# The last cycles of a six-layer attention stack in an order of their own, with the output's normalisation inside them

## The chip, the core and the metric

One core of one Trainium2 chip runs the whole kernel. The core has five engines with a queue of instructions each: PE (matrix multiplication and transposes; its weight loads run beside it), ACT (functions and copies), DVE (vector arithmetic and reductions), POOL (vector arithmetic, slower) and SP, which here only issues DMAs. They meet through semaphores. The metric is the device time of one execution in microseconds; lower is better. A measurement of this kernel is uncertain by about 0.2%.

## What is computed

The input x is 8 sequences of 512 tokens of 128 numbers. The reference, cut to what matters:

```
x = x + layernorm(L0_attn_ref(layernorm(x), Wq, ..., bo))
x = x + layernorm(L0_ffn_ref(layernorm(x), Wqkv, ..., b2))

# L0_ffn_ref
for i in range(6):
    x = attn_layer(shift_tokens(x), Wqkv[i], q_scale[i], k_scale[i], Wo[i]) + x
    x = ffn_layer(shift_tokens(x), ln_g[i], ln_b[i], W1[i], b1[i], W2[i], b2[i]) + x
```

`attn_layer` has 16 heads of 64: q and k are normalised, turned by rotary tables, and each window of 32 tokens looks at itself and the window before. `ffn_layer` is a layer normalisation, a gated product with an exact gelu and a second product. What the change touches is the end: the last cycles of layer 6, and the last line, the normalisation of the stack's result and the addition of the residual.

## The kernel before

The kernel has three stages: `mqa_stage` (the first attention; it also writes its result, the residual, to DRAM), `layers_stage` (the six layers) and `output_stage`. Inside the layers, x stays in SBUF, transposed, as `xT`.

**Cycles.** A tile is 128 tokens; a sequence has 4 tiles, a half has 2 (`PER`). A cycle works on one half at each of many steps, so a layer has 16 cycles (`STEPS`) and a sequence two. The table `CYCLE` writes down, engine by engine, in what order the steps of a cycle stand, each with the tile that it is for, counted from the cycle's first:

```
CYCLE = {
    "PE": "Tq:0 aPq:2 mean bPq:2 Tk:0 V:-2 aPk:2 var bPk:2 S:0 spread X:-1 aPv:2 O:-2 bPv:2 Tq:1 V:-1 Tk:1 "
    "aPq:3 O:-1 bPq:3 GG S:1 AA aPk:3 bPk:3 W:-1 aPv:3 X:0 bPv:3 F4",
...
    "DVE": "XC aCq:2 bCq:2 Rq:2 FV R:-2 aCk:2 XM bCk:2 MX:0 RS:-1 SB:0 R:-1 Rk:2 aCq:3 bCq:3 MX:1 Rq:3 AM "
    "aCk:3 bCk:3 WX:-1 RS:0 SB:1 XN Rk:3",
```

In the text, a step's number is its tile or half in the last layer: S:30 is S for tile 30 of 0 to 31 (cycle 15 is the one that begins with Tq:30), XN:14 is the FFN's last step for half 14. The steps on PE: P projects to q, k, v (three matmuls each, into `proj`); Tq and Tk transpose q and k; S makes the scores (128 pairs of weight load and matmul of 64x64); X transposes the probabilities; V weights the values (128 such pairs); O transposes the attention's result; W is the output projection. The FFN follows two cycles behind (`LAG`): mean, var and spread for its normalisation, GG and AA the two halves of the first product, F4 the second. On the others: DVE has C and R of the rotation and l2 norm, MX and SB before the exponential, RS the denominators, R the weighting, WX and XN the two additions to `xT`, XC, FV, XM, AM in the FFN; ACT copies out of PSUM (EQ, EK, EX, EO, EV, XF, XH) and computes EXP and GEL; POOL has A, M, N of the rotation and norms, FP (a power of -1/2), XL and Xl; SP has VM, which moves a tile's values to `v_win` by ten DMAs.

**What sets the order.** Each engine runs its row of the table in order, and a step first waits for its inputs' semaphores. The outputs of most steps of PE go to a ring of two PSUM tensors (`ring`, `take`), so a step also waits until the reader of the last user of its slot is done (`RELEASE`). `steps_of` leaves out, at both ends, the steps whose tile does not exist: so the last cycles are the same row with gaps. PE runs its cycles in a loop (`Fori`) up to cycle 13 of the last layer; cycles 14 to 17 stand behind it as straight code. The other engines have loops of their own (`run`, `middle`), which end there too. At the end of each layer's turn of its loop SP loads the next layer's weights (`new_layer`), which in the sixth layer there is nothing of.

**The output stage** starts behind a barrier of all engines. SP loads the whole residual (2 MB) in one DMA. PE transposes all 8 sequences into 8 PSUM banks. Then, per sequence, DVE computes statistics and variance, POOL the power -1/2, DVE the normalised tiles, POOL adds them to the residual, and SP sends it out. The steps of one sequence stand beside those of the next.

## Time and profile before

| | us |
|---|---|
| median of three runs | 3441.85 (3436.19 to 3443.91) |
| the profiled execution | 3438.51 |
| its span, first to last instruction | 3436.8 |
| PE busy | 3273.3 (95%) |
| DVE busy | 2964.5 (86%) |
| ACT busy | 2734.5 (80%) |
| POOL busy | 2616.0 (76%) |
| mean granted TensorE clock | 0.984 of full speed |

A profile is one execution: each instruction has a start and a duration, from the span's start. "Busy" is the time in which an engine had an instruction under way. The idle time ahead of an instruction stands in brackets with what ended it; "issue" means that the profile shows nothing that the engine waited for. PEld is PE's weight load. The granted clock is 1.00 at full speed and 0.50 when PE runs at half of it.

### The profile page before, as it was taken

To read this page: it belongs to the slowest core of one execution; us is meant where nothing else is said; L and a number is where in the kernel's file an instruction comes from. 1 tells how busy PE (TensorE), PEld (TensorE's weight loads), DVE (VectorE), ACT (ScalarE), POOL (GpSimd) and SP (SyncE) were. 2 spreads that over 40 slices of the span, in tenths; PEclk is the share of its full clock that TensorE was granted. 3 is DMA by queue.
4 is the path that set the end of the run, shared out by engine and by line. 5 is a ranking of instruction groups with operands and counts; after the bars stand their busy time and mean duration, and the time that the engine had idled before them with its cause. 6 is when DMAs were issued, how large, how long until landed. Compare 5 with 4: busy or idle time off the path is not lost. (4 is left out here: it accounts for less than half of the span.)

```text
span 3436.8 us, 161363 instructions
## 1 busy us (share of the span) xinstructions
PE 3273.3 (95%) x66105; PEld 2798.2 (81%) x66106; DVE 2964.5 (86%) x5351; ACT 2734.5 (80%) x4522; POOL 2616.0 (76%) x3358
## 2 busy tenths in 40 slices
PE   7999679999999999999999999999999999999994
PEld 5767458888888888888888888888888888888883
DVE  7777578999999999989999999999999999999974
ACT  4777458888888888888888888888888888888872
POOL 5677577777887777887778787778778778778762
PEclk9999889999999999999999999999999999999997
DMA  2000013222223222232222232222232222222221
GB/s 61 4 8 8 16 51 99 74 69 66 64 77 99 73 70 65 71 94 74 73 73 62 74 92 73 73 73 61 75 92 73 73 73 68 69 66 73 73 67 59
DMA packets 161797, 228.61 MB, mean 67 GB/s; under 512 B 42264, under 2 KB 60640, under 8 KB 161504
## 3 DMA queue, kind: packets, MB, share of 16 engines
q1 hardware_dynamic: 161632, 226.85, 24.6%
q8 instruction: 49, 0.80, 0.1%
q14 instruction: 116, 0.95, 0.1%
HBM read 21.00 MB, written 4.19 MB: 7 GB/s over the span
## 5 line engine op out<-in xcount | busy, mean ns | idle before, releaser
L1184 POOL TENSOR_TENSOR by_cos<-by_cos,by_sin 128x1024 f32<-128x1024 f32 x384 | 913.9, 2390 | 0.0
L1190 POOL TENSOR_TENSOR by_cos<-by_cos,norms 128x1024 f32<-128x1024 f32 x384 | 729.6, 1911 | 0.0
L1560 DVE TENSOR_TENSOR by_cos<-proj,turns 128x512 f32<-128x512 f32 x768 | 523.9, 682 | 72.3 <-ACT squares L1446 67.9
L1289 PE MATMUL proj<-qkv_hi,xs_hib 128*128 128x512 f32 x1152 | 559.7, 486 | 25.7 <-DVE by_sin L1562 12.9
L1562 DVE TENSOR_TENSOR by_sin<-proj,turns 128x512 f32<-128x512 f32 x768 | 521.5, 679 | 0.0
L1446 ACT ACTIVATE squares<-proj 128x512 f32<-128x512 f32 x768 | 443.1, 592 | 42.7 <-DVE sumsb L1566 16.1
L1566 DVE TENSOR_REDUCE sumsb<-squares 128x16 f32<-128x1024 f32 x384 | 464.1, 1209 | 0.0
L1291 PE MATMUL proj<-qkv_hi,xs_lob 128*128 128x512 f32 x1152 | 458.9, 398 | 0.7 <-issue 0.7
L1290 PE MATMUL proj<-qkv_lo,xs_hib 128*128 128x512 f32 x1152 | 456.2, 396 | 0.0
L1298 PE MATMUL ring<-ident,by_cos 128*128 128x128 f32 x3072 | 405.9, 275 | 8.8 <-ACT pTb L1425 4.5
L1298 PEld LDWEIGHTS ring<-ident,by_cos 128*128 128x128 f32 x3072 | 351.5, 141 | 57.7 <-issue 9.6
L1352 PE MATMUL ring<-attnT,wo 128*128 128x256 f32 x1536 | 347.2, 379 | 0.6 <-ACT hidden L1529 0.6
L1317 PEld LDWEIGHTS score<-kTb,qTb 64*32 64x32 f32 x24576 | 278.9, 105 | 62.8 <-issue 40.3
L1352 PEld LDWEIGHTS ring<-attnT,wo 128*128 128x128 f32 x1536 | 291.7, 190 | 43.7 <-ACT hidden L1529 0.8
L1317 PE MATMUL score<-kTb,qTb 64*32 64x64 f32 x24576 | 320.8, 226 | 4.2 <-issue 3.9
L1425 ACT ACTIVATE pTb<-ring 128x1024 f32<-128x1024 f32 x192 | 196.9, 1026 | 160.3 <-PE ring L1324 157.3
L1168 POOL TENSOR_TENSOR newton_b<-norms 128x32 f32<-128x32 f32 x384 | 91.8, 239 | 294.4 <-ACT norms L1457 279.4
L1425 ACT ACTIVATE qTb<-ring 128x1024 f32<-128x1024 f32 x192 | 197.0, 1026 | 139.4 <-PE ring L1298 139.3
L1338 PE MATMUL ring<-v_win,pTb 64*32 64x64 f32 x24576 | 286.6, 226 | 9.3 <-issue 9.3
L742 DVE CUSTOM_DVE_ANT_0 a_masked<-a_score,a_mask_qk 128x512 f32<-128x512 f32 (+3 forms) x512 | 229.5, 487 | 72.3 <-PE a_score L390 65.0
L1338 PEld LDWEIGHTS ring<-v_win,pTb 64*32 64x32 f32 x24576 | 254.8, 105 | 42.7 <-issue 42.7
L1575 DVE TENSOR_REDUCE row_maxb<-score 128x16 f32<-128x1024 f32 x192 | 234.0, 1219 | 52.6 <-PE score L1317 52.5
(190 smaller groups left out, 7850.3 us busy)
## 6 DMA issues: line engine op xcount, KB each, us to landing
v_win<-vb SPq DMA_DIRECT2D x1152, 128.0 KB
v_win<-vb SPq DMA_DIRECT2D x768, 64.0 KB
in_qkv<-L_ffn_Wqkv SPq DMA_DIRECT2D x12, 768.0 KB
wo<-L_ffn_Wo SPq DMA_DIRECT2D x6, 512.0 KB, 4.1
x_tok<-L_attn_x SPq DMA_DIRECT2D x8, 256.0 KB, 4.4
residual<-x_tok SPq DMA_DIRECT2D x8, 256.0 KB, 2.0
o_x<-residual SPq DMA_DIRECT2D x1, 2048.0 KB, 8.5
out<-o_x SPq DMA_DIRECT2D x8, 256.0 KB, 2.2
```

The source lines that it names most:

```text
L1184: nc.gpsimd.tensor_tensor(both, both, by_sin[:, j, :], ALU.add).then_inc(e[f"{w_}_added"].sem, 1)
L1190: nc.gpsimd.tensor_tensor(heads, heads, inverse, ALU.mult).then_inc(e[f"{w_}_ready"].sem, 1)
L1289: nc.tensor.matmul(out, xs_hi[:, tile], qkv_hi[:, cols], start=True, stop=False)
L1290: nc.tensor.matmul(out, xs_hi[:, tile], qkv_lo[:, cols], start=False, stop=False)
L1291: nc.tensor.matmul(out, xs_lo[:, tile], qkv_hi[:, cols], start=False, stop=True)\
L1298: last = nc.tensor.transpose(out[:, i * P:(i + 1) * P], by_cos[:, t % 2, j, i * P:(i + 1) * P], ident[:, :])
L1317: last = nc.tensor.matmul(score[queries, at:at + KEYS], qT[rows, t % 2, i, queries], keys, start=False, stop=True, skip_group_check=True)
L1338: last = nc.tensor.matmul(out[queries, at:at + DH], pT[rows, i, queries], v_win[rows, t % 2, n, i, :], start=True, stop=True)
L1352: last = nc.tensor.matmul(out[:, 0:HS], wo[:, i, :], attnT[:, i, :], start=(i == 0), stop=(i == PAIRS - 1))
L1560: nc.vector.tensor_tensor(of_heads(by_cos[:, t % 2, j, cols]), heads, table(0), ALU.mult)
L1562: nc.vector.tensor_tensor(swapped, heads, table(1), ALU.mult).then_inc(e[f"{w_}_rotated"].sem, 1)
L1566: nc.vector.tensor_reduce(sums[:, t % 2, j, :, 0], squares[:, :].rearrange("p (h d) -> p h d", d=DH), AX.X, ALU.add).then_inc(e[f"{w_}_sum ...
```

## The change

Two things are put together. First, the last layer's last cycles no longer come from `CYCLE` with gaps: a new table, `LAST`, has a row of its own for each engine for all that is left from cycle 15 on, with the same steps in nearly the same order. `last_steps` reads it. Cycle 14 now is the last one of `CYCLE`, and on PE it runs in the loop, which goes one cycle further. Second, `output_stage` is gone. Its work is cut in nine units (`UNITS`): sequences 0 to 6, and the two halves of sequence 7. Five kinds of step of each stand inside the rows of `LAST`: Y (PE transposes the unit's tiles into one half of `proj`, by turns), YS (DVE: statistics and variance), YR (POOL: power), YN (DVE: normalised into a half of `squares`), YA (POOL: addition). Y:u waits, from u = 2 on, until YN:(u-2) is done. The residual is loaded by SP once the last layer's weights have been converted, into the space of the loaded weights and of the rotary tables (`in_qkv`, `tables`): two DMAs, 2 MB together, at the place where other layers load weights. The additions are made there, and the outputs sent from there as units become ready, behind all of SP's VM steps. There is no barrier between the layers and the output.

The core of the diff:

```diff
+UNITS = [(b, 0, TILES) for b in range(B - 1)] + [(B - 1, h * PER, PER) for h in range(HALVES)]
+LAST = {
+    "PE": "Tq:30 mean:13 Y:0 Y:1 Tk:30 V:28 var:13 S:30 spread:13 X:29 O:28 Tq:31 V:29 Tk:31 Y:2 O:29 GG:13 "
+    "S:31 AA:13 W:29 X:30 F4:13 mean:14 Y:3 V:30 var:14 spread:14 X:31 O:30 GG:14 V:31 O:31 Y:4 AA:14 W:31 Y:5 "
+    "F4:14 mean:15 Y:6 var:15 spread:15 GG:15 Y:7 AA:15 F4:15 Y:8",
...
+}
...
-def layers_stage(nc, c, e, w, arrived):
+def layers_stage(nc, c, e, w, arrived, residual, out_dram):
...
+            last_layer()
             middle(DEPTH - 1)
-            for at in range(STEPS - HALVES, STEPS + HALVES * LAG):
-                cycle(((DEPTH - 1) * STEPS, at), None, DEPTH - 1, at, 0, PER * STEPS)
+            base = (DEPTH - 1) * STEPS
+            for at in range(STEPS - HALVES, STEPS - 1):
+                cycle((base, at), None, DEPTH - 1, at, 0, PER * STEPS)
+            for at, s_, t, token in last_steps(name):
+                step(s_, t, token, (base, at), None, DEPTH - 1)
...
+            def last_layer():
+                for x in p_lo:
+                    sp.wait_ge(p_lo[x], DEPTH)
+                sp.wait_ge(p_turns, DEPTH * 4)
+                sp.sem_inc(sp_ready, 1)
+                sp.dma_start(in_qkv[:, :].rearrange("p (n d) -> p n d", d=D), residual[:, 0:AT_ONCE * TILES, :])\
+                    .then_inc(x_loaded, 16)
...
+            run(sp, "SP", step, new_layer, last_layer)
+            for u, (b, first, n) in enumerate(UNITS):
+                sp.wait_ge(summed, u + 1)
+                sp.dma_start(out_dram[b].rearrange("(t p) d -> p t d", p=P)[:, first:first + n, :],
+                             residual_of(u).rearrange("p (t d) -> p t d", d=D)).then_inc(stored, 16)
...
+                elif kind == "YR":
+                    n = UNITS[t][2]
+                    pool.wait_ge(var_done, t + 1)
+                    nc.gpsimd.tensor_tensor(o_rstd[:, t % 2, 0:n], o_var[:, t % 2, 0:n], c["minus_half"][:, 0:n],
+                                            ALU.pow).then_inc(rstd_done, 1)
+                elif kind == "YA":
+                    pool.wait_ge(x_loaded, 32)
+                    pool.wait_ge(normalised, t + 1)
+                    nc.gpsimd.tensor_tensor(residual_of(t), residual_of(t), normal_of(t), ALU.add).then_inc(summed, 1)
...
+                elif kind == "Y":
+                    b, first, n = UNITS[t]
+                    half = HALVES * b + (first + n) // PER - 1
+                    pe.wait_ge(e["x_new"].sem, e["x_new"].at(half + 1, (DEPTH - 1) * STEPS))
+                    if t < 2:
+                        pe.wait_ge(e["v"].sem, e["v"].at(PER * STEPS, (DEPTH - 1) * STEPS))
+                    else:
+                        pe.wait_ge(normalised, t - 1)
+                    for i in range(n):
+                        at = 1 + (first + i) * P
+                        last = nc.tensor.transpose(turned_of(t)[:, i * P:(i + 1) * P], c["xT"][:, b, at:at + P], ident[:, :])
+                    last.then_inc(turned, 1)
...
-            with nc.Fori(LAG, DEPTH * STEPS - HALVES, engines=one, hint_back_edge=True) as n:
+            with nc.Fori(LAG, DEPTH * STEPS - 1, engines=one, hint_back_edge=True) as n:
                 cycle(n)
...
+                elif kind == "YN":
+                    dve.wait_ge(rstd_done, t + 1)
+                    if t >= 2:
+                        dve.wait_ge(summed, t - 1)
+                    for i in range(UNITS[t][2]):
+                        tile = slice(i * P, (i + 1) * P)
+                        last = nc.vector.tensor_scalar(normal_of(t)[:, tile], turned_of(t)[:, tile], stat[:, t % 2, i, 0:1],
+                                                       o_rstd[:, t % 2, i:i + 1], ALU.subtract, ALU.mult)
...
-def output_stage(nc, c, residual, out_dram):
...
-        layers_stage(nc, c, layers, ffn_inputs, arrived)
-        output_stage(nc, c, residual, out_dram)
+        layers_stage(nc, c, layers, ffn_inputs, arrived, residual, out_dram)
```

The rows of `LAST` of the other engines, for cycle 16 and 17 (from XN:13 on DVE): "XN:13 XC:14 SB:31 FV:14 R:30 XM:14 RS:31 YN:2 R:31 YS:3 YS:4 YN:3 AM:14 YN:4 WX:31 YS:5 XN:14 XC:15 FV:15 XM:15 YN:5 YS:6 YS:7 AM:15 YN:6 XN:15 YS:8 YN:7 YN:8"; ACT: "XF:14 EX:30 FSQ:14 EXP:31 XH:14 EX:31 EO:30 GEL:14 EO:31 XF:15 FSQ:15 XH:15 GEL:15".

Three places of the order that results. PE where its loop ends, before (`COMPARE_AND_BRANCH` is the loop's end; L1289 to L1291 with `proj` are the projections, L1298 is Tq or Tk, L1338 V, L1362 mean, L1393 F4):

```order
L1393 MATMUL ring<-hidden,w 128x256 x3
L1415 REGISTER_ALU
L1415 COMPARE_AND_BRANCH
L1298 MATMUL ring<-ident,by_cos 128x128 x8
L1289 MATMUL proj<-qkv_hi,xs_hib 128x512
L1290 MATMUL proj<-qkv_lo,xs_hib 128x512
L1291 MATMUL proj<-qkv_hi,xs_lob 128x512
L1362 MATMUL ring<-xfb,mean_of 128x256
```

and PE where its loop ends, after the change (L1376 is Tq or Tk, L1443 is Y, L1416 V, L1458 var, L1395 S, L1465 spread):

```order
L1505 COMPARE_AND_BRANCH
L1376 MATMUL ring<-ident,by_cos 128x128 x8
L1452 MATMUL ring<-xfb,mean_of 128x256
L1443 MATMUL proj<-ident,xT 128x128 x8
L1376 MATMUL ring<-ident,by_cos 128x128 x8
L1416 MATMUL ring<-v_win,pTb 32x64 x64
L1458 MATMUL ring<-mean_of,fsqb 128x1 x2
L1395 MATMUL score<-kTb,qTb 32x64 x64
L1465 MATMUL ring<-ident,f_rstdb 128x128 x2
```

Cycle 14, with its projections, is no longer behind the loop; what follows it is cycle 15, with the transposes of Y:0 and Y:1 ahead of Tk:30.

PE in cycle 16, before: from spread:14 over X:31, O:30, V:31, O:31 to the first rows of GG:14.

```order
L1375 MATMUL ring<-ident,f_rstdb 128x128 x2
L1324 MATMUL ring<-ident,probs 128x128 x8
L1345 MATMUL ring<-ident,attnb 128x128 x8
L1338 MATMUL ring<-v_win,pTb 32x64 x64
L1345 MATMUL ring<-ident,attnb 128x128 x8
L1384 MATMUL ring<-xn_hib,w_hi 128x256
```

and after the change, from O:30 over GG:14 (the rows L1474 to L1476, of which there are nine), V:31, O:31 and Y:4 to the first row of AA:14:

```order
L1423 MATMUL ring<-ident,attnb 128x128 x8
L1474 MATMUL ring<-xn_hib,w_hi 128x256
...
L1416 MATMUL ring<-v_win,pTb 32x64 x64
L1423 MATMUL ring<-ident,attnb 128x128 x8
L1443 MATMUL proj<-ident,xT 128x128 x4
L1474 MATMUL ring<-xn_hib,w_hi 128x256
```

GG:14 has moved ahead of V:31, and Y:4 stands behind O:31.

DVE at the program's end, after the change: from XM:15 (L1741) over YN:5 (L1723), YS:6 and YS:7 to AM:15 (L1749), YN:6, XN:15 (L1755) and the last unit.

```order
L1741 TENSOR_TENSOR xcb<-xcb,ring 128x256
L1723 TENSOR_SCALAR squares<-proj,o_stat,o_rstd 128x128 x4
L1708 BN_STATS o_stat<-proj 128x6 x4
L1712 BN_AGGR o_stat<-o_stat 128x2 x4
L1715 TENSOR_SCALAR o_var<-o_stat 128x4
...
L1749 SCALAR_TENSOR_TENSOR hidden<-ring,ffn_col,hidden 85x256
L1723 TENSOR_SCALAR squares<-proj,o_stat,o_rstd 128x128 x4
L1755 TENSOR_TENSOR xT<-ring,xT 128x256
L1708 BN_STATS o_stat<-proj 128x6 x2
L1712 BN_AGGR o_stat<-o_stat 128x2 x2
L1715 TENSOR_SCALAR o_var<-o_stat 128x2
L1723 TENSOR_SCALAR squares<-proj,o_stat,o_rstd 128x128 x4
```

Before, XM:15, AM:15 and XN:15 followed each other directly, and all eight sequences' statistics stood behind XN:15; now only the last unit's do, and the normalisation of the last two.

## Rows read from the trace of the kernel before

**Rows 1.** Chain that ended last, in order of time: start us, us, what.

```profile
3404.31 8.49 DMA o_x<-residual
...
3432.87 1.27 POOLq L1647
```

**Rows 2.** Timeline of the output stage: start us, us, engine, line, operation, out<-in, count [idle].

```profile
3404.82 3.22 PE L1666 MATMUL o_turn<-ident,xT 128*128 128x128 f32 x28
...
3417.89 0.88 DVE L1690 BATCH_NORM_STATS2 o_stat<-o_turn 128x6 f32<-128x128 f32 x4
...
3418.80 0.38 DVE L1694 BATCH_NORM_AGGREGATE o_stat<-o_stat 128x2 f32<-128x6 f32 x4
3419.22 0.17 DVE L1697 TENSOR_SCALAR o_var<-o_stat 128x4 f32<-128x4 f32 x1
3419.31 1.37 DVE L1703 TENSOR_SCALAR o_o<-o_turn,o_stat,o_rstd 128x128 f32<-128x128 f32 x4
3419.47 1.02 POOL L1676 TENSOR_TENSOR o_rstd<-o_var,minus_half 128x4 f32<-128x4 f32 x1 [0.16 <-DVE o_var L1697]
```

**Rows 3.** Busy us by stretch, XN to XN: cycles 15, 13, 14, 16, 17.

```profile
3329.90:3359.80 29.90, 24.70 (x624) 21.90 (x621) 13.81 (x20) 17.89 (x23) 8.63 (x14) 0.89 0.28 73
3267.40:3297.30 29.90, 29.90 (x661) 26.21 (x660) 27.36 (x41) 25.47 (x40) 23.52 (x30) 1.00 0.27 71
3297.30:3329.90 32.60, 30.62 (x663) 26.34 (x662) 27.41 (x41) 24.84 (x38) 23.70 (x29) 1.00 0.26 68
3359.80:3390.20 30.40, 20.04 (x328) 16.85 (x328) 6.93 (x14) 9.80 (x15) 1.97 (x3) 0.72 0.01 2
3390.20:3403.60 13.40, 7.13 (x32) 5.62 (x32) 2.66 (x8) 4.98 (x8) 1.98 (x3) 0.75 0.00 0
```

(The columns: stretch, its us, then PE, PEld, DVE, ACT, POOL with their instructions, granted clock, DMA share, GB/s.)

**Rows 4.** The page's groups: S (L1317) and V (L1338), busy, mean ns | idle.

```profile
L1317 PE MATMUL score<-kTb,qTb 64*32 64x64 f32 x24576 | 320.8, 226 | 4.2 <-issue 3.9
...
L1338 PE MATMUL ring<-v_win,pTb 64*32 64x64 f32 x24576 | 286.6, 226 | 9.3 <-issue 9.3
```

**Rows 5.** Timeline of PE: the waits for "issue" inside S and V.

```profile
3307.88 0.32 PE L1317 MATMUL score<-kTb,qTb 64*32 64x64 f32 x10 [1.27 <-issue]
...
3335.49 0.43 PE L1338 MATMUL ring<-v_win,pTb 64*32 64x64 f32 x24 [1.34 <-issue]
...
3339.56 0.67 PE L1317 MATMUL score<-kTb,qTb 64*32 64x64 f32 x29 [1.94 <-issue]
...
3365.26 0.37 PE L1338 MATMUL ring<-v_win,pTb 64*32 64x64 f32 x2 [1.96 <-issue]
...
3376.55 0.66 PE L1338 MATMUL ring<-v_win,pTb 64*32 64x64 f32 x26 [2.42 <-issue]
```

**Rows 6.** Timelines of PE, POOL and DVE in cycles 15 to 17.

```profile
3331.84 1.09 PE L1298 MATMUL ring<-ident,by_cos 128*128 128x128 f32 x8 [0.74 <-ACT qTb L1425]
...
3384.32 3.72 PE L1352 MATMUL ring<-attnT,wo 128*128 128x256 f32 x16 [0.57 <-ACT hidden L1529]
3388.55 1.56 PE L1393 MATMUL ring<-hidden,w 128*128 128x256 f32 x6 [0.52 <-DVE xT L1603]
...
3393.24 0.71 POOL L1213 TENSOR_TENSOR f_rstdb<-f_varb,minus_half 128x2 f32<-128x2 f32 x1 [20.77 <-DVE f_varb L1622]
...
3396.87 0.55 PE L1384 MATMUL ring<-xn_hib,w_hi 128*128 128x256 f32 x1 [2.17 <-POOL xn_lob L1209]
...
3400.61 1.26 DVE L1634 SCALAR_TENSOR_TENSOR hidden<-ring,ffn_col,hidden 128x256 f32<-128x256 f32 x3 [5.46 <-PE ring L1386]
3403.59 0.42 DVE L1640 TENSOR_TENSOR xT<-ring,xT 128x256 f32<-128x256 f32 x1 [1.72 <-PE ring L1393]
```

**Rows 7.** Timeline of SP in a layer before: the weights' load, and the next VM.

```profile
2503.02 0.87 SPq L936 DMA_DIRECT2D in_qkv<-L_ffn_Wqkv  x2
...
2516.74 0.55 SPq L1128 DMA_DIRECT2D v_win<-vb  x1
```

**Rows 8.** POOL's additions in the output stage: ns min/median/max, first and last start.

```profile
L1682 POOL TENSOR_TENSOR o_x<-o_x,o_o x8: 1259/1260/1262, 3415.4 to 3432.9; 128x512 f32<-128x512 f32 x8
```

**Rows 9.** The page's DMA issues: the outputs, KB each, median us to landing.

```profile
out<-o_x SPq DMA_DIRECT2D x8, 256.0 KB, 2.2
```

More of the change, by code:

```diff
@@ L906, in steps_of, with last_steps @@
     return steps
+def last_steps(engine):
+    at = STEPS - 1
+    for token in LAST[engine].split():
+        name, _, n = token.partition(":")
+        if name in OUTPUT:
+            yield at, (name,), int(n), ""
+            continue
+        same = [(t, x) for x, kind, t in tokens(engine) if kind == name and (name in FFN or (int(n) - t) % PER == 0)]
+        t, steady = same[0]
+        at = int(n) + LAG if name in FFN else (int(n) - t) // PER
+        yield at, (name,), t, steady
 def layer_events(sem):
```

109 lines of the change are left out of this document (41 added, 68 removed), and 8 rows, old and new, of the table LAST.

## The prediction

> **What bounds the kernel now.** Three views, in this order. First the chain that ended last: it shows that behind the last cycle stands a stage of its own, from 3404.01 us (end of the last XN [rows 6]) to the span's end at 3436.8, so 32.8 us. It begins with a wait of 8.49 us for the DMA that fetches the residual [rows 1], and then goes round eight times: statistics, variance, power, normalisation, addition, on DVE and POOL by turns, while PE and ACT do nothing. The eight additions begin between 3415.4 and 3432.9, so a round is 2.5 us (its parts are in [rows 2, 8]). Second the busy time by stretch, cut at the XN of each cycle [rows 3]: cycle 13, the last that PE takes from its loop, has 29.90 us with PE busy all through. Cycle 14 has the same number of matmuls, but 32.60. From cycle 15 on PE is no longer full (24.70 of 29.90, then 20.04 of 30.40, then 7.13 of 13.40), because the pipeline runs empty: each step waits for the one before it. There is free time on every engine, DVE above all (13.81 of 29.90, 6.93 of 30.40). Third the idle time put down to "issue" on PE [rows 4, 5], below.
>
> **The wait for instructions.** Over the whole run S waited 3.9 us for "issue" in 24576 matmuls and V 9.3 us [rows 4], and most of that lies behind PE's loop: 1.27 and 1.94 in S, 1.34, 1.96 and 2.42 in V [rows 5]. Between the stall at the pair 105 of V:28 and the one at pair 100 of S:30 stand 24 + 4 + 99 pairs and two waits: 256 instructions (a pair is a weight load and a matmul). All five stalls fit a mark every 256 instructions, of which one is 570 behind the loop's exit, at pair 119 of S:28. The closest two stalls end 4.1 us apart (3335.49 to 3339.56), and a tile of V or S, 256 instructions, takes only some 1.5 to 1.8 us without one. So a mark costs 1.3 to 2.4 us where V or S lies between it and the last one, and nothing elsewhere. In the loop there is no such wait.
>
> The Trainium skill, "Runtime: NRT & Kernel Launch", section "Instruction fetch mechanics", has the same 256 instructions (16 KiB blocks, the next fetched while one is executed), and says that passing a block costs little, "mostly hidden". The rows disagree on the cost: 1.3 to 2.4 us each. By the page the term for cycle 14 below would be nought and the marks without a price (rival E).
>
> **The change, part by part.** All against the profiled execution (span 3436.8).
> 1. The output stage goes: -32.8.
> 2. What comes behind XN:15 instead is the half-sequence unit 8. Two transposes and their delay 0.4; two statistics (4 take 0.88), two aggregates (4 take 0.38) and the variance 0.17, with gaps 1.0 (half of a round's, the variance whole); power of 128x2, 0.71 as the FFN's [rows 6]; normalisation of two tiles, half of 1.37, 0.7; addition of 128x256, between half of 1.26 and that, taken 0.7; output DMA and end, as now from 3434.14 (end of the last addition) to 3436.8, 2.7 [rows 1, 2, 8]. With five hand-overs of 0.07 us: +6.6. YN:7 (0.7) lies beside the power, YA:7 beside YN:8. Bounds: 6 to 8.5, if they do not.
> 3. Cycle 14 of PE now runs in the loop (the loop ends one cycle later). The twin of it is cycle 13: 32.60 - 29.90 = -2.7; I take -2.5, since some of the first stalls stay behind the exit. Bounds -2.7 and 0, the latter if the stalls hit cycle 15 instead and nothing covers them.
> 4. Cycle 15. Y:0 and Y:1 (28 transposes took 3.22 us, so 0.5 us for four, 0.6 with their delay) come ahead of Tk:30, which waited 0.74 us for ACT's copy [rows 2, 6]: +0.4. Y:2 stands ahead of O:29, which waits for DVE's R:29: nothing. With the Y's the marks of 256 fall elsewhere. Counted on the rows of the order: at the last pair of V:28, pair 122 of S:30, pair 94 of V:29, pair 62 of S:31 (long after the last one: free). Three stalls, of 1.9, 1.9 and about 1, instead of 1.34 and 1.94: +1.5, of which the waits for ACT and DVE in Tq:31 and O:29 take some: +0.6. Together +1.0, between 0 and +3.
> 5. Cycle 16. The mark moves to pair 13 of V:30 with nothing dense before it, so V:30's 1.96 goes, less Y:3's 0.5 ahead of it: -1.4. V:31 keeps a stall of about 1.9 (pair 107). GG:14 goes from behind O:31 to ahead of V:31, and XH:14 ahead of EX:31 on ACT: GG and AA together lie between 3396.87 and AM's 3400.61 in the last cycle [rows 6], so GG alone costs up to 1.9 us; I take it that V:31 starts 1.5 us later, but behind O:31 stand only Y:4 and AA:14 instead of GG and AA, and W:31 no longer waits for the gelu (0.57 [rows 6]). Net of that move -0.6. Sum -2.0, but a V:31 that is late by more takes it back: between -4.5 and +1.
> 6. The end of cycle 16: Y:5 (0.6 us) comes between W:31 and F4:14, YS:5 (1.4) on DVE between WX:31 and XN:14. F4 started 0.5 us behind W's end (3388.04 to 3388.55) and takes 1.6 [rows 6], which covers both but for a little: +0.2. SB:31 behind XC:14, YN:3 and YN:4 lie in idle time of DVE.
> 7. Cycle 17: YN:5, YS:6 and YS:7 (1.4 + 1.5 + 0.8 = 3.7) must fit in the 5.46 us that DVE is idle before AM:15, YN:6 (1.4) in the 1.72 before XN:15 [rows 6]; both fit. Y:7 between GG and AA: +0.3. If that cover fails, each us is a us.
> 8. The residual's load, 2 MB in 8.49 us, moves to cycle 4 of the last layer, on SP's queue ahead of VM. It waits for events that are past by then. At that place the other layers load Wqkv and the FFN's weights: issued from 2503.02, next VM at 2516.74 [rows 7]. The 13.7 us cover the 8.5. Cost 0; if they did not, VM and V behind it would be late once, by 1 or 2 us. The outputs 0 to 6 leave SP beside PE's work, at 2.2 us each [rows 9]: 0.
>
> On POOL the additions (1.26) and powers (1.02) go into idle time: POOL is busy 8.63 of 29.90 and 1.97 of 30.40 us there [rows 3]. POOL's additions last 1259 to 1262 ns in all eight rounds [rows 8], the last one with DVE idle, the others beside its statistics, so I add nothing. If they were slowed beside DVE's additions in the cycles, only the last two have a waiting reader.
>
> The clock: the granted share is 0.89, 0.72 and 0.75 in the last three stretches [rows 3], that is PE falls to the lower of its levels (1.2 instead of 2.4 GHz) after its idle stretches. I take it that it does so as often. If the Y's keep PE busier at the right moments, or the stalls lie worse, transposes, W, GG and AA of cycle 16 and 17 (some 20 us of PE) take up to 3 us less or 5 more.
>
> Sum: -32.8 + 6.6 - 2.5 + 1.0 - 2.0 + 0.2 + 0.3 = -29.2. Span 3407.6. The profiled execution took 3438.5, 1.7 over its span and 3.3 under the median of the three runs (3441.85); the four times shown (3436.2 to 3443.9) have a mean of 3440.1. I set the change against that mean: 3410.9, and 0.6 for the register and wait instructions of the new steps: 3411.5.
>
> **Rivals.**
> A. *The tail becomes denser.* V:30 and V:31 both escape their marks and the clock stays up: XN:15 comes 4 to 8 us earlier. For it: cycle 16 has 10 us of idle PE, and V:31, R:31 and O:31, one behind the other, set its end. Against: the count above puts a mark in V:31. 3403 to 3407.
> B. *The stalls and the clock eat it.* Five marks in dense places instead of four, the Y's in front of V, and the slow clock over W:31 and GG:15 (W 3.7 us now, twice that at 1.2 GHz): 5 to 10 us later. 3416 to 3422.
> C. *Slower than before.* The Y's have two halves of proj, and Y:u waits on PE, in order, for the normalisation of u-2. If that wait ran the full chain each time (transposes 0.6, statistics 1.5, power 1.02, normalisation 1.37 = 4.5 us, a little more at the lower clock, and all of PE's work behind it), the seven units that wait would cost 32 to 36 us, against 29.2 saved: 3443 to 3447. It decides with the seventh unit. Against: each Y stands several us of other work behind the YN that it waits for; DVE and POOL have the time.
> D. *It does not do what it says*: the gain of the stage given back by item 2 being as long as now, since the addition or output queues behind the earlier ones on SP. At 2.2 us per DMA and one issue each 0.4 us I see only 1 or 2 us: inside the range.
>
> E. *The marks have no price.* If the waits for "issue" were chance and not code that has to come, cycle 14 would keep its 32.6 us in the loop too, and items 3 to 5 would come to nought but for the Y's: -32.8 + 6.6 + 0.8 (item 4 and 5's Y's) + 0.5 = -24.9, 3415 to 3416. Against: 256 between them, five times.
>
> **How the numbers follow.** Forecast (3407 to 3415) 0.62, A 0.14, B 0.15, C 0.01, E 0.05, something that leaves it within 7 us of before (D among it) 0.03. The range, A's and B's middle included and the 4 us between executions of one kernel: 3403 to 3420. A measurement tells about 0.2% (7 us) from no change: faster 0.96, same 0.03, slower 0.01.
>
> **What would show it.** Cycle 14 in 30 us instead of 32.6 (item 3). "Issue" before S and V only behind that, at the pairs named. No wait of DVE for a power ahead of MX:31, AM or XN. From XN:15's end to the span's end 6.6 us. The out DMAs of units 0 to 5 before cycle 17. PE waiting in Y for normalised would make it wrong, and so would XN:14 more than 2 us later than now, set against XN:12.

## Result, and the profile after

The changed kernel took 3408.79 us (median of four executions, 3406.70 to 3409.57), the kernel before beside it 3442.88 us (3436.19 to 3447.51): ratio 0.9897, 95% interval 0.9885 to 0.991. The profiled execution took 3406.7 us, its span is 3405.0 (before: 3438.5 and 3436.8). The prediction was 3411.5, between 3403 and 3420. The stretches did not come out as it said, though: its terms for cycles 15 and 16 were wrong in size, in opposite directions, and that they nearly cancel in the sum is luck.

Busy time by stretch in the changed kernel, from XN to XN: cycles 13 to 17, then all that stands behind the start of XN:15. The columns are those of [rows 3].

```profile
3264.30:3294.20 29.90, 29.90 (x662) 26.10 (x661) 27.37 (x41) 25.50 (x40) 23.53 (x30) 1.00 0.27 71
3294.20:3324.50 30.30, 30.30 (x663) 26.42 (x662) 27.39 (x41) 24.88 (x39) 23.71 (x29) 1.00 0.26 70
3324.50:3360.30 35.80, 27.75 (x636) 24.60 (x633) 19.55 (x55) 17.26 (x23) 14.11 (x19) 0.81 0.28 76
3360.30:3384.30 24.00, 18.32 (x340) 15.30 (x340) 15.99 (x53) 10.15 (x16) 5.41 (x7) 0.93 0.04 13
3384.30:3398.40 14.10, 8.27 (x38) 6.82 (x38) 7.61 (x30) 4.98 (x8) 8.59 (x10) 0.76 0.18 56
3398.40:3405.00 6.60, 0.44 (x2) 0.21 (x2) 2.63 (x10) 0.00 (x0) 3.04 (x4) 0.74 0.25 79
```

Against [rows 3]: cycle 14 has 30.3 instead of 32.6, cycle 15 35.8 instead of 29.9 (1.0 more was forecast), cycle 16 24.0 instead of 30.4 (2.0 less was forecast), with a granted clock of 0.93 where it was 0.72. POOL and DVE now do the output's work in cycles 15 to 17 (DVE 19.55 and 15.99 instead of 13.81 and 6.93). Behind the start of XN:15 stand 6.6 us instead of 33.2. The last 3.1 us of the 31.8 by which the spans differ lie ahead of cycle 14, where PE's order was not edited: the first addition to `xT` (the first WX; the expectations below call it the first XN) stands 1.4 us sooner, the layers from there up to cycle 13 take 1.7 less.

The page's groups of S and V in the changed kernel (busy, mean ns | idle before), for [rows 4]; S waits less for "issue", V more:

```profile
L1395 PE MATMUL score<-kTb,qTb 64*32 64x64 f32 x24576 | 320.9, 226 | 1.9 <-issue 1.5
...
L1416 PE MATMUL ring<-v_win,pTb 64*32 64x64 f32 x24576 | 286.3, 226 | 10.4 <-issue 10.3
```

The waits themselves, from PE's timeline, for [rows 5] (start, us, [idle ahead of it]):

```profile
3330.33 2.02 PE L1416 MATMUL ring<-v_win,pTb 64*32 64x64 f32 x127 [2.75 <-issue]
3334.09 0.26 PE L1416 MATMUL ring<-v_win,pTb 64*32 64x64 f32 x1 [1.74 <-issue]
3338.46 0.43 PE L1395 MATMUL score<-kTb,qTb 64*32 64x64 f32 x6 [1.23 <-issue]
3347.47 0.54 PE L1416 MATMUL ring<-v_win,pTb 64*32 64x64 f32 x35 [2.21 <-issue]
3372.15 0.42 PE L1416 MATMUL ring<-v_win,pTb 64*32 64x64 f32 x22 [1.75 <-issue]
```

A group "x35" is the last 35 pairs of a tile of 128, so it begins at pair 94. The last four stand where the prediction put them, to within one pair (last pair of V:28, pair 123 of S:30 for 122, pair 94 of V:29, pair 107 of V:31), and V:30 and S:31 have none. The first, 2.75 us ahead of V:28, was not forecast. It is the mark at 58 instructions behind the loop's exit, which had cost nothing in the trace of before.

The end of the program, from the timeline of all engines:

```profile
3398.33 0.42 DVE L1755 TENSOR_TENSOR xT<-ring,xT 128x256 f32<-128x256 f32 x1 [0.45 <-PE ring L1483]
3398.81 0.21 PEld L1443 LDWEIGHTS proj<-ident,xT 128*128 128x128 f32 x2 [0.92 <-DVE xT L1755]
...
3399.29 0.49 DVE L1708 BATCH_NORM_STATS2 o_stat<-proj 128x6 f32<-128x128 f32 x2 [0.54 <-PE proj L1443]
...
3400.35 0.71 POOL L1283 TENSOR_TENSOR o_rstd<-o_var,minus_half 128x2 f32<-128x2 f32 x1 [1.06 <-DVE o_var L1715]
...
3401.97 0.72 POOL L1288 TENSOR_TENSOR tables_sb<-tables_sb,squares 128x256 f32<-128x256 f32 x1 [0.19 <-DVE squares L1723]
```

One unit goes through the chain that eight sequences went through before [rows 2]: transposes 3398.81, addition at 3401.97, span's end 3405.0.

One sign that the prediction named did not come: of the output DMAs of units 0 to 5 only three were issued before cycle 17 (3355.57, 3357.35 and 3377.73 us), the next three in it (3386.42 to 3393.25). Nothing waits for them but the end of the program, which the last unit's sets.

### The profile page after: what moved, and what is told of

It is laid out like the page before. It is cut to its first block, busy times and chain, and to the rows that moved or that the text cites. A ratio compares the mean times of both kernels' runs of the same rounds, so it can differ in the third digit from the quotient of the medians.

```text
span 3405.0 us, 161393 instructions
## 1 busy us (share of the span) xinstructions
PE 3269.8 (96%) x66106; PEld 2794.3 (82%) x66106; DVE 2966.7 (87%) x5352; ACT 2734.6 (80%) x4522; POOL 2616.7 (77%) x3360
## 4 chain that ended last, share of the span: by engine, by line
POOL 38%; issue 32%; PE 15%; POOLq 2%; DVE 1%; ACT 1%; SPq 0%; DVEq 0%; ACTq 0%; DMA 0%
POOL by_cos L1253 12%; POOL by_cos L1259 9%; POOL newton_b L1239 2%; POOL newton_b L1241 2%; POOL norms L1243 2%; POOL newton_b L1237 2%; POOL xs_lob L1267 2%; POOL xn_lob L1278 2%; PE ring L1376 2%; POOL f_rstdb L1291 2%; PE ring L1430 2%; PE score L1395 1%; PE ring L1416 1%; PE proj L1367 1%; POOLq L1059 1%
## 5 line engine op out<-in xcount | busy, mean ns | idle before, releaser
L1376 PE MATMUL ring<-ident,by_cos 128*128 128x128 f32 x3072 | 405.5, 275 | 7.8 <-ACT pTb L1518 4.5
L1376 PEld LDWEIGHTS ring<-ident,by_cos 128*128 128x128 f32 x3072 | 351.4, 141 | 56.4 <-issue 9.4
L1395 PEld LDWEIGHTS score<-kTb,qTb 64*32 64x32 f32 x24576 | 278.9, 105 | 59.9 <-issue 37.2
L1395 PE MATMUL score<-kTb,qTb 64*32 64x64 f32 x24576 | 320.9, 226 | 1.9 <-issue 1.5
L1416 PE MATMUL ring<-v_win,pTb 64*32 64x64 f32 x24576 | 286.3, 226 | 10.4 <-issue 10.3
L1416 PEld LDWEIGHTS ring<-v_win,pTb 64*32 64x32 f32 x24576 | 254.5, 105 | 41.5 <-issue 41.3
```

What stands on the lines that cost most here:

```text
L1376: last = nc.tensor.transpose(out[:, i * P:(i + 1) * P], by_cos[:, t % 2, j, i * P:(i + 1) * P], ident[:, :])
L1395: last = nc.tensor.matmul(score[queries, at:at + KEYS], qT[rows, t % 2, i, queries], keys, start=False, stop=True, skip_group_check=True)
L1416: last = nc.tensor.matmul(out[queries, at:at + DH], pT[rows, i, queries], v_win[rows, t % 2, n, i, :], start=True, stop=True)
```

## Experiments

All were measured beside runs of the kernel before, in five sessions, not all on one chip; the medians of the kernel before lie between 3442.88 and 3443.80 us in all of them. "Tail" is the time from the start of XN:11 (the end of cycle 13) to the span's end, in one trace; "marks" is the sum of the waits for "issue" at marks in it; the waits of 0.56 and 1.22 ahead of V:30's and V:31's first pairs in cycle 16, there in both traces of before, are not among them, nor are 0.27 and 0.35 ahead of V:29 in e9 and e11 (no code block was under way at any of these: the last packet had left 7.5 to 10.3 us before they ended). "Ahead" says whether the first code block behind PE's loop was fetched before the exit (16 KB packets of PE's instruction queue in the trace). Each tail is that of one traced execution, and it need not be the median one: e1's was the slowest of its nine (3441.89 us) and e5's of its four, the changed kernel's first and e10's were the fastest of their four.

| kernel | median us (n) | tail | cycle 14 | 15 and 16 | 17 | from XN:15 | marks | ahead |
|---|---|---|---|---|---|---|---|---|
| before | 3442.88 (4) | 139.5 | 32.6 | 60.3 | 13.4 | 33.2 | 9.6 | yes |
| before again, e8 | 3443.07 (1) | 143.5 | 36.2 | 60.5 | 13.5 | 33.2 | 11.0 | no |
| changed | 3408.79 (4) | 110.8 | 30.3 | 59.8 | 14.1 | 6.6 | 9.7 | no |
| changed again, e9 | 3409.56 (4) | 108.5 | 30.3 | 57.4 | 14.2 | 6.6 | 7.8 | yes |
| e1 loop only | 3435.95 (9) | 139.0 | 30.2 | 61.3 | 15.1 | 32.4 | 7.1 | no |
| e2 all behind | 3435.83 (11) | 136.6 | 30.3 | 58.1 | 13.7 | 34.6 | 5.5 | no |
| e6 behind, four | 3429.46 (7) | 129.8 | 30.4 | 58.7 | 13.7 | 27.0 | 6.3 | no |
| e3 GG late | 3412.33 (4) | 113.8 | 30.2 | 62.5 | 14.1 | 6.9 | 9.1 | no |
| e7 short loop | 3412.43 (4) | 111.2 | 35.5 | 54.8 | 14.2 | 6.7 | 9.1 | no |
| e4 shift at start | 3408.45 (4) | 104.9 | 30.3 | 52.2 | 15.5 | 6.9 | 4.3 | no |
| e5 shift spread | 3398.47 (4) | 104.6 | 30.3 | 51.9 | 15.5 | 6.9 | 3.9 | no |
| e10 the same again | 3398.19 (4) | 101.4 | 30.3 | 48.7 | 15.5 | 6.9 | 3.0 | yes |
| e12 shift by 28 | 3405.61 (4) | 104.8 | 30.3 | 53.8 | 14.1 | 6.6 | 7.0 | no |
| e11 no hint | 3405.41 (4) | 106.8 | 30.3 | 56.0 | 13.9 | 6.6 | 8.0 | (kept) |

**The longer loop alone (e1).** Before, with

```
-            with nc.Fori(LAG, DEPTH * STEPS - HALVES, engines=one, hint_back_edge=True) as n:
+            with nc.Fori(LAG, DEPTH * STEPS - 1, engines=one, hint_back_edge=True) as n:
...
-            for at in range(STEPS - HALVES, STEPS + HALVES):
+            for at in range(STEPS - 1, STEPS + HALVES):
```

> The kernel before with one edit: PE's loop ends one cycle later, so that cycle 14 of the last layer runs in it; output stage and order as before. Theory (stalls for code at marks of 256 instructions, the first 58 behind the loop's exit): cycle 14 takes 30.3 us instead of 32.6. The marks behind the exit then fall at pair 9 of V:28, pair 3 of S:30, the start of X:29, pair 103 of V:29 and pair 75 of S:31, and at sparse places from there on: stalls of about 2.7, 1.9, 1.9 and 0.9 us in cycle 15 and none in V:30 and V:31, where before had 1.96 and 2.42. Cycle 15 longer by 4, cycle 16 shorter by 4 us. In all -2.5 us against before. Rival (the first mark is free when no Y stands in front of V:28, as it was in before): no stall at V:28, cycle 15 longer by 1.5 only, in all -5 us. Rival (the wait moves with V's and S's, not with the marks): V:30 and V:31 keep their 1.96 and 2.42.

Measured: 3435.95 us, ratio to before 0.9976 (0.9966 to 0.9986), so 5 to 12 us less by the interval: more than the theory's 2.5, with the rival's 5 at its edge. The marks are where the count put them. PE's timeline of e1:

```profile
3337.26 1.97 PE L1338 MATMUL ring<-v_win,pTb 64*32 64x64 f32 x120 [2.62 <-issue]
3341.13 2.03 PE L1317 MATMUL score<-kTb,qTb 64*32 64x64 f32 x125 [0.61 <-issue]
3345.26 1.87 PE L1324 MATMUL ring<-ident,probs 128*128 128x128 f32 x8 [1.49 <-issue]
3353.99 0.66 PE L1338 MATMUL ring<-v_win,pTb 64*32 64x64 f32 x26 [2.42 <-issue]
```

So V:28 is stalled without any Y in front of it: "the first mark is free" falls, and so does "the wait moves with V and S". The size was explained only by e8: set against its tail of 143.5, e1's 139.0 is 4.5 us less.

**The kernel before once more (e8).**

> The kernel before once more, for a second trace: how much of the difference between two traces lies in stretches that no edit touches. From the span's start to the first XN and from there to the last layer's cycle 13 the traces so far (without the one with 104 increments at the start) differ by 4 and by 3 us. Expected: the stalls for issue at the same pairs as in the first trace of this kernel (pair 118 of S:28, 105 of V:28, 100 of S:30, V:30 and V:31), their lengths within 0.7 us, and the stretch from XN:12 to the end 105 to 109 us, moved by the granted clock. The other reading (stalls for issue are chance) would put them elsewhere.

Measured: 3443.07 us. PE's timeline of this second trace:

```profile
3304.00 1.47 PE L1338 MATMUL ring<-v_win,pTb 64*32 64x64 f32 x126 [2.40 <-issue]
3307.47 0.79 PE L1291 MATMUL proj<-qkv_hi,xs_lob 128*128 128x512 f32 x1 [0.85 <-issue]
...
3340.00 0.43 PE L1338 MATMUL ring<-v_win,pTb 64*32 64x64 f32 x24 [1.61 <-issue]
3343.80 0.67 PE L1317 MATMUL score<-kTb,qTb 64*32 64x64 f32 x29 [1.67 <-issue]
```

Pair 105 of V:28 and pair 100 of S:30 again. But S:28 has none, and at pair 3 of V:26, the mark at 58 behind the exit, stand 2.40 us that the first trace did not have. In the first trace the block behind the exit was fetched at 3295.48, 1.6 us ahead of the exit; in this one at 3301.38, when PE came to the mark. Cycle 14 took 36.2 us here and 32.6 there. The prediction sized its term for cycle 14 on the rarer of two cases: of the 14 traces it is in three, the other one in ten, and in e11 the block needed no fetch.

**Only the order of GG:14 (e3).** PE of the changed kernel, with XH:14 and GEL:14 put back on ACT too:

```
-    "S:31 AA:13 W:29 X:30 F4:13 mean:14 Y:3 V:30 var:14 spread:14 X:31 O:30 GG:14 V:31 O:31 Y:4 AA:14 W:31 Y:5 "
+    "S:31 AA:13 W:29 X:30 F4:13 mean:14 Y:3 V:30 var:14 spread:14 X:31 O:30 V:31 O:31 Y:4 GG:14 AA:14 W:31 Y:5 "
```

> The changed kernel with GG:14 put back behind O:31 and Y:4 on PE, and XH:14 behind EX:31 and GEL:14 behind EO:31 on ACT, as in the kernel before; all else as in the changed one. Theory (the record's -0.6 us for this move): total +0.6 us, V:31 starts about 1.5 us sooner and W:31 waits 0.5 us for the gelu again; XN:13 to XN:14 24.5 us instead of 23.9. Rival (the move is what brought cycle 16 its 6.4 us, by keeping PE busy between V:30 and V:31 and its clock up): XN:13 to XN:14 27 us or more, granted clock well under 0.93 there, total +3 or more. Rival (V:31's start sets the end): total -1 us.

Measured: 3412.33 us (3409.28 to 3414.21, the changed kernel 3406.70 to 3409.57), its tail 3.0 longer, cycle 16 26.1 instead of 23.9; of the rest, 0.6 lies in cycle 15, ahead of the edit's place on PE. PE's timeline, first e3, then the changed kernel, at V:31:

```profile
3371.32 1.04 PE L1417 MATMUL ring<-ident,attnb 128*128 128x128 f32 x8
3374.10 1.38 PE L1410 MATMUL ring<-v_win,pTb 64*32 64x64 f32 x116 [1.75 <-ACT attnT L1512]
...
3382.22 0.41 PE L1469 MATMUL ring<-xn_lob,w_hi 128*128 128x256 f32 x1
```

```profile
3366.51 1.04 PE L1423 MATMUL ring<-ident,attnb 128*128 128x128 f32 x8
3367.85 0.39 PE L1474 MATMUL ring<-xn_hib,w_hi 128*128 128x256 f32 x1 [0.30 <-ACT pTb L1518]
...
3369.10 1.30 PE L1416 MATMUL ring<-v_win,pTb 64*32 64x64 f32 x106
```

V:31 waits 1.75 us for ACT's copy of O:30 when nothing stands in front of it. GG:14 fits into that wait: from O:30's start to V:31's start are 2.78 us without GG and 2.59 with it. The prediction had V:31 come 1.5 us later for it, although the first trace of the kernel before has a wait at the same place, put down to "issue" there:

```profile
3372.92 1.21 PE L1338 MATMUL ring<-v_win,pTb 64*32 64x64 f32 x102 [1.22 <-issue]
```

Behind O:31, GG and AA run 14 of their 18 matmuls at 0.41 us each, at the lower clock, where the changed kernel has mostly 0.28. The stalls' places and sums are nearly the same (9.1 and 9.7), so the 2.2 us of cycle 16 are GG's place with the clock there (0.87 instead of 0.93), by one trace of each.

**All the output behind XN:15 (e2), and with four places (e6).** e2 keeps the early load of the residual, has no stage and no barrier, and puts the 45 output steps last; all other steps stand in the order of the kernel before, GG:14 behind O:31 too (cut):

```
-    "F4:14 mean:15 Y:6 var:15 spread:15 GG:15 Y:7 AA:15 F4:15 Y:8",
+    "F4:14 mean:15 var:15 spread:15 GG:15 AA:15 F4:15 Y:0 Y:1 Y:2 Y:3 Y:4 Y:5 Y:6 Y:7 Y:8",
...
+    "AM:15 XN:15 YS:0 YS:1 YN:0 YS:2 YN:1 YS:3 YN:2 YS:4 YN:3 YS:5 YN:4 YS:6 YN:5 YS:7 YN:6 YS:8 YN:7 YN:8",
```

> The changed kernel with the nine output units Y, YS, YR, YN, YA all behind XN:15, and everything else in the last cycles in the order of the kernel before. The residual is still loaded in cycle 4 of the last layer and there is no stage boundary. Theory: the 8.5 us of waiting for the residual go, the eight rounds stay, so XN:15's end to the span's end is 24 to 25 us instead of 32.8 (before) and 6.3 (after); up to XN:15 as the kernel with the longer loop alone. Total about 11 us under before, near 3430 us, 22 us over after. Rival (the load is not what sets it, since the first statistics run beside it anyway): 29 to 30 us behind XN:15, total near 3435. Rival (Y's two halves of proj cost a full chain of 4.5 us each): 36 us or more behind XN:15, total at or over before's.

Measured: 3435.83 us, the same as e1, and 34.1 us from XN:15's end, so the early load brought nothing here. A round in e2's timeline, the first Y that has to wait and the next:

```profile
3402.91 1.09 PE L1437 MATMUL proj<-ident,xT 128*128 128x128 f32 x4 [3.94 <-DVE squares L1717]
3404.03 0.89 DVE L1702 BATCH_NORM_STATS2 o_stat<-proj 128x6 f32<-128x128 f32 x4 [1.27 <-PE proj L1437]
...
3406.96 1.08 PE L1437 MATMUL proj<-ident,xT 128*128 128x128 f32 x4 [2.96 <-DVE squares L1717]
```

A round is 4.06 us, because Y:u stands behind the normalisation of u-2. This is rival C's chain (4.5 us by its estimate), measured where nothing covers it. e6 uses four places of PSUM, and the first four units also wait until `score` is free (cut):

```
-            return proj[:, u % 2 * 512:u % 2 * 512 + UNITS[u][2] * P]
+            return (proj, score)[u // 2 % 2][:, u % 2 * 512:u % 2 * 512 + UNITS[u][2] * P]
...
-                        pe.wait_ge(normalised, t - 1)
+                        pe.wait_ge(normalised, t - 3)
```

> The kernel with all output units behind XN:15, but with four places in PSUM for the turned tiles (the two halves of proj and the two of score) instead of two, so that Y:u waits for the normalisation of unit u-4. With two places XN:15's end to the span's end took 34.1 us: seven waits on PE of 3 us, a round of 4.06 us. Theory (the two places were what ate the 8.5 us of the early load): rounds at DVE's pace, 2.8 to 2.9 us, 26 to 27.5 us behind XN:15, total 7 us under the kernel with two places. Rival (the addition's or the power's wait on POOL sets the round): unchanged, 34 us. The record's 6.6 us behind XN:15 is not touched by either.

Measured: 3429.46 us, 26.5 us from XN:15's end, rounds of 2.70 us. So the early load and the missing barrier are worth 32.8 - 26.5 = 6.3 us once Y's wait no longer sets the round, two places of PSUM instead of four take 7.6 (34.1 - 26.5), and having all but unit 8 inside the cycles is worth the remaining 20.3 (26.5 to 6.2).

**The short loop (e7).** The changed kernel with cycle 14 as straight code again:

```
-            with nc.Fori(LAG, DEPTH * STEPS - 1, engines=one, hint_back_edge=True) as n:
+            with nc.Fori(LAG, DEPTH * STEPS - HALVES, engines=one, hint_back_edge=True) as n:
...
+            cycle((DEPTH - 1) * STEPS + STEPS - HALVES, STEPS - HALVES, 0, PER * STEPS)
```

> The changed kernel with PE's loop ending one cycle sooner, as in the kernel before: cycle 14 of the last layer is straight code again. By the record (cycle 14 is worth 2.5 us, all else stays): 2.5 us slower than the changed kernel. Theory now (the sum of the stalls counts, and the marks move by 1344 instructions modulo 256): cycle 14 takes 32.6 us again, but the marks fall at pair 95 of V:28, pair 90 of S:30, pair 61 of V:29, pair 29 of S:31, X:30, pair 108 of V:30 and pair 74 of V:31, and the first mark behind the loop's exit was fetched ahead in the kernel before, so V:28 loses its 2.75 and pays 1.2 to 1.3; S:30 1.9, V:29 0 to 1, V:30 and V:31 nearly nothing. Stalls 6 to 7 us in all instead of 9.7: 3 us faster than the changed kernel, near 3405.5. If the first mark behind the exit is paid whole here too, at pair 2 of V:26, it is even.

Measured: 3412.43 us (3411.36 to 3415.96), 3.6 over the changed kernel's median and 2.9 over e9's, with no overlap: the theory (3 us faster) was wrong. Its tail is 0.4 longer than the changed kernel's first and 2.8 longer than its second. Cycle 14 costs 5.2 more, cycles 15 and 16 give 4.9 back (V:28's start is not stalled). Of what the loop gains in cycle 14, most is paid again behind the exit.

**Moving the marks (e4, e5, e10, e12).** Semaphore increments that nobody waits for, on PE ahead of its loop. e4 has 104 at the program's start:

```
+            for _ in range(104):
+                pe.sem_inc(pad, 1)
```

> The changed kernel with 104 more instructions on PE (semaphore increments that nobody waits for) at the very start of the program, where PE is idle until 9.8 us. Theory (blocks of 256 instructions at fixed places of the code): every mark behind the loop's exit comes 104 instructions sooner in the sequence of steps, or 152 later: pair 76 of V:28, pair 70 of S:30, pair 42 of V:29, pair 10 of S:31, the start of W:29, pair 89 of V:30, pair 55 of V:31. Stalls: V:28 up to 2.75, S:30 1.7, W:29 1, none in V:29, V:30 and V:31; in all 5.4 us instead of 9.7, total -4 us, near 3404.5. Rival (the marks are counted from the loop's exit): all stalls where they were (V:28 start, its last pair, pair 123 of S:30, pair 94 of V:29, pair 107 of V:31), total unchanged. Rival (no marks, chance): unchanged in sum, other places.

Measured: 3408.45 us, no gain. But the program's start paid for it. Its first row on PE, and the waits at the marks (e4's timeline):

```profile
16.93 1.09 PE L375 MATMUL a_near<-ident,a_xnb 128*128 128x128 f32 x4 [16.93 <-issue]
...
3339.51 1.07 PE L1419 MATMUL ring<-v_win,pTb 64*32 64x64 f32 x59 [2.25 <-issue]
3343.15 1.18 PE L1398 MATMUL score<-kTb,qTb 64*32 64x64 f32 x64 [0.52 <-issue]
3356.57 0.39 PE L1477 MATMUL ring<-xn_hib,w_hi 128*128 128x256 f32 x1 [0.56 <-issue]
3366.98 0.70 PE L1419 MATMUL ring<-v_win,pTb 64*32 64x64 f32 x46 [0.98 <-issue]
```

16.9 instead of 9.8 us ahead of the first matmul, and all marks moved (the places are some 6 pairs short of the count, for which there is no explanation): 4.3 us of stalls, a tail of 104.9 instead of 110.8. The increments stand 0.151 us apart in its trace. e5 divides the same 104 among three places at which PE is idle anyway:

> The changed kernel with the same 104 semaphore increments on PE, but 36 at the program's start, 34 ahead of the mask's matmuls of the layers and 34 behind them, three places at which PE is idle for 9.8, 7.0 and 7.0 us. In the run with all 104 at the start the first matmul came at 16.9 instead of 9.8 us (0.16 us each), while XN:12 to the span's end took 74.6 instead of 80.5 us. Theory: the three idle stretches hide 34 to 36 increments each (5.8 us), the stalls behind the loop stay as in that run, so the total is about 6 us under the changed kernel, near 3402.5 us, and the first XN stands where it does in the changed kernel. Rival (the increments cost their 7 us wherever they stand, or the shorter tail was a matter of that execution's clock): near 3408, no gain.

Measured: 3398.47 us (3396.02 to 3401.30). The first WX stands at 505.1 us, in the changed kernel at 505.3. Marks (e5's timeline), now at the counted places to within one pair, pair 76 of V:28, 71 of S:30, W:29 and 89 of V:30:

```profile
3331.27 0.96 PE L1421 MATMUL ring<-v_win,pTb 64*32 64x64 f32 x53 [1.89 <-issue]
3334.88 1.13 PE L1400 MATMUL score<-kTb,qTb 64*32 64x64 f32 x58 [0.46 <-issue]
3348.78 3.69 PE L1435 MATMUL ring<-attnT,wo 128*128 128x256 f32 x16 [0.36 <-issue]
3358.70 0.65 PE L1421 MATMUL ring<-v_win,pTb 64*32 64x64 f32 x40 [1.19 <-issue]
```

Then the changed kernel and this one again, on one chip:

> The changed kernel once more, beside the shifted one on the same chip, with a second trace. Expected: 3408 to 3410 us; the stalls for issue at the same pairs as in its first trace (start of V:28, its last pair, pair 123 of S:30, pair 94 of V:29, pair 107 of V:31), 8.5 to 10.5 us in all; XN:12 to the span's end 79.5 to 82 us. If the first mark behind the loop's exit was fetched ahead this time, as in one of the two traces of the kernel before, V:28's start has no stall and the stretch is 3 us shorter.

> The kernel with the 104 increments in three idle places once more, beside the changed kernel on the same chip. The first time it took 3398.5 us, its trace 3399.6, with 3.9 us of stalls where the changed kernel has 9.7. By the stalls and XN:12 to the end (74.2 against 80.5 us) it should be 6 us faster than the changed kernel; the medians of different chips said 10. Theory: 6 us, ratio 0.9982, 3402 or so where the changed kernel has 3408 to 3409. Rival (the shift brings something else besides, in the stage before the layers, where the marks move too): 10 us again, with the first XN or the layers sooner.

Measured: 3409.56 us (3407.53 to 3409.72) and 3398.19 us (3395.26 to 3401.29): 11.4 us or 0.33% less, with no overlap. In these two traces the first block came ahead of the exit, so V:28's mark cost nothing in either, and the tails are 108.5 and 101.4, 7.1 apart (6.2 between the two that had the late fetch). Cycle 16 has the full clock in the shifted kernel's traces (1.00 instead of 0.93), while cycle 17 gives 1.4 us back (clock 0.68 instead of 0.76). Two or three us more come ahead of the first WX, by the few traces there are; the wait for "issue" on PE shortly ahead of it (at 481 to 496 us) is 1.2 and 1.4 us there, 1.9 in the changed kernel's first trace and 1.7 and 1.8, two of them, in its second. The rest is not settled. e12 shifts by 28:

> The changed kernel with 28 increments at the program's start (PE idle for 9.8 us, 28 at 0.16 us are 4.5) instead of none. A shift as such should bring nothing, only the places that the marks get. By the count they fall at the first transposes of Y:0 or Y:1, pair 114 of V:28, pair 108 of S:30, pair 80 of V:29, pair 48 of S:31, Y:3 or the start of V:30, pair 127 of V:30, pair 93 of V:31. Theory: stalls of 2.2 to 2.7, 1.7, 1.9, 0 to 1, 0, 0, 1.9 and 1, in all 9 to 10 us as in the changed kernel, total within 2 us of it, 3407 to 3411. Rival (increments ahead of the loop help for another reason, as the 10 us of the shifted kernel against 6 in its tail suggest): 2 us or more faster.

Measured: 3405.61 us (3402.76 to 3409.51): the median is 3 us less, though the theory said even, but the executions overlap with the changed kernel's (3406.70 to 3409.57), so this is not clear of noise. Its marks hit the places (transposes of a Y 2.41, pair 114 of V:28 1.01, pair 109 of S:30 1.61, pair 127 of V:30 2.01); the one in V:31 is free. The marks are 2.6 us less than in the changed kernel's first trace, but the tail is 6.0 less. What else differs is the clock, in cycle 15 (rows of e12, then of e9, where X:29 and O:28 stand behind S:30's stall):

```profile
3331.10:3360.40 29.30, 23.86 (x636) 20.92 (x634) 19.68 (x55) 17.31 (x23) 14.27 (x19) 1.00 0.35 93
...
3343.43 1.04 PE L1407 MATMUL ring<-ident,probs 128*128 128x128 f32 x8
```

```profile
3329.78:3363.31 33.53, 27.20 (x636) 24.26 (x634) 19.59 (x55) 17.29 (x24) 14.17 (x19) 0.85 0.31 81
...
3340.44 0.43 PE L1395 MATMUL score<-kTb,qTb 64*32 64x64 f32 x6 [1.80 <-issue]
...
3341.28 1.91 PE L1402 MATMUL ring<-ident,probs 128*128 128x128 f32 x8
3342.99 1.52 PE L1423 MATMUL ring<-ident,attnb 128*128 128x128 f32 x8
```

**Without the hint (e11).** `hint_back_edge=False` on PE's loop, in the changed kernel.

> The changed kernel without the hint on the branch back at the end of PE's loop. In 2 of the 11 traces with a place for it to show (the kernel before, the changed kernel's second; the shifted one's second is a third) the first block behind the loop's exit was fetched 1.7 us ahead of the exit, in the others only when PE came to the first mark. If the hint is what keeps the code behind the exit from being fetched: no stall at V:28's start, and what lies behind it as in the second trace of the changed kernel, 3 us less in the tail; the loop may pay for it at each of its 93 passes, each 0.1 us there being 9 us in all. If the hint has nothing to do with it: as the changed kernel, 3407 to 3410, V:28's start stalled by 2.2 to 2.8.

Measured: 3405.41 us (3404.43 to 3412.45). The loop pays nothing (2789.3 us from the first XN to XN:11, 2788.9 and 2791.5 in the changed kernel's traces). In its trace V:28's start has no stall, and no block was fetched at the exit at all; the next mark costs 1.56 us, ahead of var:13. Instead the trace has one code packet more in the loop's first pass: its last ones ahead of the exit are at 530.6 and 534.8 us, the changed kernel's at 522.8 and 528.0, and both traces have 43 in all. So the block behind the loop was most likely loaded then and kept for the 93 passes. This is one trace, and the time does not tell: one of the four executions took 3412.

**How long a mark waits, and why (all 14 traces).** The code packets' times show it without a further run. At all 62 waits of marks behind the loops the block's packet had left 2.2 to 3.0 us before the wait ended. So the wait is what is left of these 2.2 to 3.0 us when PE comes to the mark. At V:31 of the kernel before the packet left at 3374.33, when PE was there already: 2.42 us. At the free mark in S:31 of the changed kernel it left at 3349.38, by an estimate 2.9 us ahead (the tile starts at 3351.61 and takes 1.75 us, the mark is at pair 62). Nearness of the last mark is not the condition: from the end of V:30's wait to the start of V:31's are 8.9 us in the kernel before, from S:30's to V:29's 6.8 us in the changed kernel, and both cost over 2 us. In both the packet left only when the tile of V was well under way. What sets the moment at which it leaves was not tested.

## Why the prediction was right, point by point

1 and 2, the stage and unit 8. Right: 32.8 us went, and from XN:15's end to the span's end are now 6.2 us, forecast 6.6, because the chain is one of known pieces in series [rows 2]. The 0.4 are in the last piece, from the last addition's end to the span's end: 2.3 us instead of 2.7.

3, cycle 14 in the loop. The mechanism holds, the size was from one execution. It is 2.3 us by the first trace of before (forecast 2.5), 6.0 by the second. "Some of the first stalls stay behind the exit" was worth far more than the 0.2 us given to it: the block at the exit is usually fetched too late, and the mark at 58 costs 2.75 us ahead of V:28.

4, cycle 15. Wrong in size: +5.9 instead of +1.0, over its bound of 3. The failed step is the count of stalls. The prediction took three of 1.9, 1.9 and 1 us. There were four, 2.75 + 1.74 + 1.23 + 2.21 = 7.9 us against 3.3 before. The missing one is the first mark: it was left out since [rows 5] show none there, in an execution that had its block ahead. V:29's was taken at 1, as long after the last one, and is 2.21, since its packet left when PE was at the mark. Then the price of a stall left the clock out: behind S:30's, X takes 1.9 us and O 1.5 where both take 1.0 at full clock (e9 against e12). That a stall always brings the lower clock is not shown, since e12 has stalls of 2.41 and 1.61 us in cycle 15 and a clock of 1.00.

5, cycle 16. Wrong in size the other way: -6.4 instead of -2.0, past its bound of -4.5. V:30's stall went and V:31's stayed (1.75), as forecast. GG:14's move was taken as -0.6 and is -2.2 in cycle 16 by e3: the step "V:31 starts 1.5 us later" overlooked that V:31 waits for ACT's copy of O:30 anyway (1.75 us in e3), and the clock was 0.93, not 0.72. The boundary XN:13 between the two stretches also moved, so they are better taken together: -0.6 in the first traces, -3.0 between those with the early fetch, forecast -1.0 (-0.8 with item 6).

6 and 7. Right in the main: from W:31's start to XN:14 are 5.7 us instead of 5.8 (forecast +0.2), and cycle 17 has 14.1 us instead of 13.4 (forecast +0.3). These 0.7 us lie between GG:15's start and XN:15 (7.4 instead of 6.7), where Y:7 stands.

8, the load and the queues. The load left SP at 2984.40 and the next VM stands at 2998.34, with no wait charged to it; the outputs of units 0 to 5 leave between 3355.57 and 3393.25, 6 to 8 from 3399.31, and none holds up another engine. That it costs nothing rests on the trace alone, since no experiment took it away.

The clock was put at "as often slow", with 3 us less to 5 more. It went both ways, lower in cycle 15 (0.81 instead of 0.89) and higher in cycle 16 (0.93 instead of 0.72).

Like against like, the tail is 31.1 us shorter with the early fetch and 32.7 with the late one. With the early fetch the forecast of 29.2 is 1.9 short, by cycles 15 and 16 together, where GG's move alone gives 1.6 more than forecast; with the late one it is 3.5 short, by cycle 14. Of the rivals, E (marks have no price) falls with e4, e5 and e12, in which nothing but the marks' places changes behind the exit. The Trainium skill, "Runtime: NRT & Kernel Launch", "Instruction fetch mechanics", calls the crossing "mostly hidden". In these traces that holds where the packet leaves about 2.9 us or more ahead of the mark (S:31 and V:30 of the changed kernel), not where it leaves later: 0.4 to 2.75 us at 62 marks. B happened in cycle 15 and A in cycle 16, and that together they gave the middle is luck. C is shown by e2 at 4.06 us a round where nothing covers it. Inside the cycles no Y waited for a normalisation: the only idle time that the timeline has ahead of a Y behind the loop is Y:8's 0.52, for XN:15.

## What to carry to other kernels

Work hidden in a pipeline's draining cycles is worth its whole length there, but only if each piece has an engine idle in front of a wait that exists anyway: look for the wait first (V:31's 1.2 us in the trace of before), then move the step into it. Buffers that are enough inside (two places) may cost outside: 34.1 us instead of 26.5 with four. A stall on which a term rests should be looked at in a second trace of the same kernel, since the first may be of the lucky kind. And straight code behind this long loop had its own costs at fixed distances, which a hundred empty instructions in an idle place at the program's start can move: 0.33% here, more than the choice of where the loop ends.
